# Six transformer blocks over eight sequences in one fused kernel: the up projection as three fp32r products, with new orders and PSUM banks on every engine

## What is computed

```
for i in range(DEPTH):                                   # 6
    x = attn_layer(shift_tokens(x), Wqkv[i], q_scale[i], k_scale[i], Wo[i]) + x
    x = ffn_layer(shift_tokens(x), ln_g[i], ln_b[i], W1[i], b1[i], W2[i], b2[i]) + x

def ffn_layer(x, g, bln, W1, b1, W2, b2):
    xn = (x - mu) / jnp.sqrt(var + 1e-05) * g + bln
    hg = xn @ W1 + b1                                    # 128 -> 2 x 341, the up projection
    a, gate = jnp.split(hg, 2, -1)
    return a * jax.nn.gelu(gate, approximate=False) @ W2 + b2
```

## Time and profile before

| | |
|---|---|
| median of 3 runs | 1501.54 us (1500.04 to 1501.63) |
| span of the profiled execution | 1500.0 us |
| PE busy | 1464.2 us (98%) |
| DVE, ACT, POOL busy | 1310.1 (87%), 1267.7 (85%), 1248.7 (83%) us |
| PE's share of the chain that ended last | 93% |
| granted TensorE clock, mean over the span | 0.995 |

### The profile page before, as it was taken

The page is one execution under the profiler, slowest core; times in us unless marked ns, Lnnn a source line. Parts: engine busy times, 40 slices in busy tenths (PEclk is TensorE's granted clock), DMA queues, the critical chain, the costliest instruction groups (busy, mean ns, idle before and its releaser), DMA issues.

```text
span 1500.0 us, 66306 instructions
## 1 busy us (share of the span) xinstructions
PE 1464.2 (98%) x26320; PEld 1280.8 (85%) x26320; DVE 1310.1 (87%) x2365; ACT 1267.7 (85%) x2551; POOL 1248.7 (83%) x1213
## 2 busy tenths in 40 slices
PE   6799999999999999999999999999999999999997
PEld 5578888888888888888888888888888888888886
DVE  6799998889889898888898898889898988998974
ACT  4578888889888888888898888888888888888886
POOL 5489988888888888888888888888888888888781
PEclk9899999999999999999999999999999999999999
DMA  6012212111212111121211121211112121112111
GB/s 185 22 46 60 59 46 57 43 49 42 59 49 79 52 47 43 54 63 52 70 41 50 43 70 49 69 45 50 47 40 55 52 54 38 49 35 52 38 49 39
DMA packets 96184, 80.28 MB, mean 54 GB/s; under 512 B 66282, under 2 KB 79598, under 8 KB 95854
## 3 DMA queue, kind: packets, MB, share of 16 engines
q1 hardware_dynamic: 94990, 75.34, 18.8%
q10 hardware_dynamic: 864, 0.26, 0.1%
HBM read 17.91 MB, written 1.05 MB: 13 GB/s over the span
## 4 chain that ended last, share of the span: by engine, by line
PE 93%; issue 2%; DVE 2%; POOL 1%; ACT 1%; DMA 0%; ACTq 0%; DVEq 0%; POOLq 0%
PE bank L1065 74%; PE bank L1179 11%; PE bank L1217 6%; PE bank L1251 1%; PE bank L1149 1%; DMA rot<-in_b_v 0%; POOL rot L459 0%; DVE parts L891 0%; DVE newton L910 0%; DVE s L937 0%; DVE n L901 0%; DVE am L825 0%; POOL w_lo L446 0%; ACTq L550 0%; ACT rot L576 0%
## 5 line engine op out<-in xcount | busy, mean ns | idle before, releaser
L459 POOL TENSOR_TENSOR rot<-parts 128x512 f32<-128x512 f32 x384 | 493.3, 1285 | 120.4 <-DVE parts L891 120.3
L891 DVE TENSOR_TENSOR parts<-bank,rtab 128x1024 f32<-128x1024 f32 x384 | 459.8, 1208 | 0.4 <-POOL rot L459 0.3
L470 POOL TENSOR_TENSOR rot<-rot,rnorm 128x512 f32<-128x512 f32 x384 | 391.1, 1046 | 10.0 <-DVE rnorm L917 10.0
L901 DVE TENSOR_REDUCE n<-sq 128x8 f32<-128x512 f32 x384 | 257.7, 671 | 33.0 <-ACT sq L627 33.0
L689 ACT ACTIVATE pz<-bank 64x512 f32<-64x512 f32 x384 | 226.1, 589 | 61.4 <-PE bank L1217 59.1
L1065 PE MATMUL bank<-w_hi,x_hi 128*128 128x512 f32 x576 | 263.8, 458 | 4.6 <-DVE parts L891 3.6
L476 POOL TENSOR_TENSOR es<-es,r 128x512 f32<-128x512 f32 x192 | 202.6, 1055 | 75.2 <-DVE r L943 75.2
L627 ACT ACTIVATE sq<-bank 128x512 f32<-128x512 f32 x384 | 230.4, 601 | 28.0 <-DVE n L901 22.0
L1065 PE MATMUL bank<-w_hi,x_lo 128*128 128x512 f32 x576 | 229.5, 398 | 0.0
L1065 PE MATMUL bank<-w_lo,x_hi 128*128 128x512 f32 x576 | 229.1, 398 | 0.0
L1179 PE MATMUL bank<-ident,rot 128*128 128x128 f32 x1536 | 203.1, 275 | 5.0 <-POOL rot L470 2.4
(11 more groups left out here) (86 smaller groups left out, 2660.4 us busy)
## 6 DMA issues: line engine op xcount, KB each, us to landing
vb<-v SPq DMA_DIRECT2D x96, 384.0 KB, 3.8
w_new<-in_Wqkv SPq DMA_DIRECT2D x36, 256.0 KB, 4.2
vb<-v SPq DMA_DIRECT2D x48, 128.0 KB, 3.4
w_o<-in_Wo SPq DMA_DIRECT2D x12, 256.0 KB
xin<-x_tok SPq DMA_DIRECT2D x48, 64.0 KB, 2.1
xs<-x_tok SPq DMA_DIRECT2D x48, 64.0 KB, 2.0
xin<-x_tok SPq DMA_DIRECT2D x48, 56.0 KB, 2.7
xs<-x_tok SPq DMA_DIRECT2D x48, 56.0 KB, 2.0
```

The lines of the kernel that those rows point to most:

```text
L459: g.tensor_tensor(rot[:, i * CH:(i + 1) * CH].rearrange(halves, z=2, c=HD), parts[:, b:b + CH].rearrange(halves, z=2, c=HD), parts[:, b + ...
L470: g.tensor_tensor(c, c, over(r, CHH, DH), ALU.mult).then_inc(s_sc[i], 1)
L891: d.tensor_tensor(parts[:, b:b + 2 * CH].rearrange("p (w h c) -> p w h c", w=2, c=DH), heads(bank[QK_BANK[i]][:, :]).unsqueeze(1).to_broad ...
L901: d.tensor_reduce(n2[:, T * 2 * HEADS + m * CHH:T * 2 * HEADS + (m + 1) * CHH], heads(sq[:, b:b + CH]), op=ALU.add, axis=AX.X).then_inc(s_ ...
```

## The change

- The input of `hidden` is split: ACT writes xg_hi (rounded to fp32r) with `affine`, and then the same affine once more in full precision into the free half of the bank (`affine2`); DVE subtracts (`xg_lo_part`, writes xg_lo). `hidden` runs three fp32r products in the place of each fp32 product.
- W1 is loaded into w_new, and split once a layer: ACT `split_up` (w1_hi) and, for the first layer POOL, later DVE (w1_lo). There is one buffer of each for all layers. The loads of Wqkv chunks 0 and 1 come in another order around it.
- Every engine's `iteration(n)` is listed in another order, with other lags (`finish` and two of the gelus come one iteration later, DEEP is 7), and the bank tables are other ones. The counts of all other operations in a step are as before.
- PE's stream is aligned twice a step, ahead of `hidden` chunk 0 (offset 72) and ahead of `project(n, 2)` (offset 77).

```
-DEEP = 5
-BLOCK, SLOT = 256, 92
-SPLIT_FROM = 2
+DEEP = 7
+BLOCK = 256
+SPLIT_FROM = 1
...
-        w_1 = sb("w_1", 2 * 2 * HID)
+        w1_hi = sb("w1_hi", 2 * HID, F32R)
+        w1_lo = sb("w1_lo", 2 * HID, F32R)
...
+            def up_weights(l):
+                if l < DEPTH - 1:
+                    sp.wait_ge(s_wl, (l + 1) * WCH + 2 if l else 2)
+                else:
+                    sp.wait_ge(s_upl, l)
+                sp.dma_start(w_new[:, 0:2 * HID], W1[l * P:(l + 1) * P, :]).then_inc(s_up, 16)
...
-            for c in range(WCH):
+            up_weights(0)
+            for c in (2, 3, 4, 5, 0, 1):
                 qkv_weights(1, c)
...
+            def split_up(l):
+                act.wait_ge(s_up, 16 * (l + 1))
+                for j in range(HCH):
+                    act.wait_ge(s_hid[j], l * SEQS)
+                a.activation(w1_hi[:, :], w_new[:, 0:2 * HID], ACT.Copy).then_inc(s_uph, 1)
...
             def affine(n):
                 act.wait_ge(s_xnt, done(n))
                 for j in range(HCH):
                     act.wait_ge(s_hid[j], done(n - 1))
+                act.wait_ge(s_xg, n)
                 l = layer(n)
-                a.activation(xg[:, :], bank[N_BANK][:, 0:LEN], ACT.Identity, bias=shift[:, l:l + 1],
-                             scale=gain[:, l:l + 1]).then_inc(s_xg, 1)
+                a.activation(xg_hi[:, :], bank[N_BANK][:, 0:LEN], ACT.Identity, bias=shift[:, l:l + 1],
+                             scale=gain[:, l:l + 1]).then_inc(s_xgh, 1)
+
+            def affine2(n):
+                l = layer(n)
+                act.wait_ge(s_xnt, done(n))
+                a.activation(bank[N_BANK][:, LEN:2 * LEN], bank[N_BANK][:, 0:LEN], ACT.Identity, bias=shift[:, l:l + 1],
+                             scale=gain[:, l:l + 1]).then_inc(s_xgf, 1)
...
+            def xg_lo_part(n):
+                dve.wait_ge(s_xgh, done(n))
+                dve.wait_ge(s_xgf, done(n))
+                d.tensor_tensor(xg_lo[:, :], bank[N_BANK][:, LEN:2 * LEN], xg_hi[:, :].bitcast(F32), ALU.subtract)\
+                 .then_inc(s_xg, 1)
...
             def hidden(n, j):
 
                 pe.wait_ge(s_xg, done(n))
+                if n % SEQS == 0:
+                    pe.wait_ge(s_upl, layer(n) + 1)
                 for half in range(2):
-                    w = (par(n) * 2 + half) * HID + j * P
-                    last = mm(bank[H_BANK[j]][0:width(j), half * LEN:(half + 1) * LEN], w_1[:, w:w + width(j)], xg[:, :])
+                    w = slice(half * HID + j * P, half * HID + j * P + width(j))
+                    o = bank[H_BANK[j]][0:width(j), half * LEN:(half + 1) * LEN]
+                    mm(o, w1_hi[:, w], xg_hi[:, :], stop=False)
+                    mm(o, w1_lo[:, w], xg_hi[:, :], start=False, stop=False)
+                    last = mm(o, w1_hi[:, w], xg_lo[:, :], start=False)
                 last.then_inc(s_hid[j], 1)
```

More of the change, by code:

```diff
@@ L369, in later_weights @@
                     sp.wait_ge(s_xready, n)
-                for part in ((0,), (1,), (2,), (3, 4), (5, 6), (), (), ())[k]:
+                for part in ((0,), (1,), (2, 3), (4, 5), (), (), (), ())[k]:
                     weights(l, part)
             def later_qkv(n):
[L375 to L379, removed]
+                l, k = n // SEQS, n % SEQS
+                if k == 2 and l > 0:
+                    up_weights(l)
+                for c in ((), (), (), (2,), (3,), (4,), (5, 0), (1,))[k]:
+                    if l + 2 < DEPTH:
+                        qkv_weights(l + 2, c)
+            sp.wait_ge(s_zero, 3)
             def iteration(n):
@@ L961, in moments, with up_lo @@
                     d.bn_aggr(mv[:, T * 2:(T + 1) * 2], stat[:, T * 6:(T + 1) * 6]).then_inc(s_mv, 1)
+            def xg_lo_part(n):
[3 more added lines that the diff above has]
+                 .then_inc(s_xg, 1)
+            def up_lo(n):
+                if n % SEQS == SEQS - 1 and layer(n) < DEPTH - 1:
+                    dve.wait_ge(s_uph, layer(n) + 2)
+                    d.tensor_tensor(w1_lo[:, :], w_new[:, 0:2 * HID], w1_hi[:, :].bitcast(F32), ALU.subtract)\
+                     .then_inc(s_upl, 1)
             def gated(n, j):
@@ new lines, in iteration @@
+                    project_v(n - 2, 2)
+                if live(n - 1):
+                    freed((s_qte[5], n - 2), (s_rot[1], n - 1, 8, 3))
+                    project(n - 1, 7)
+                    freed((s_qte[6], n - 2), (s_rot[0], n - 1, 8, 2))
+                    project(n - 1, 6)
+                if live(n - 2):
+                    freed((s_mid[0], n - 3), (s_sub[0], n - 2, 4, 0))
+                    turn_qk(n - 2, 7)
+                if live(n):
+                    freed((s_v[3], n - 2), (s_rot[1], n - 1, 8, 1))
+                    take_in(n)
@@ new lines, in iteration @@
+                if live(n):
+                    freed((s_xl, n))
+                    project(n, 1)
+                if live(n - 2):
+                    freed((s_mid[1], n - 3), (s_qte[4], n - 2))
+                    turn_p(n - 2, 0)
+                    freed((s_pte[1], n - 2, 4, 1))
+                    freed((s_rot[1], n - 1, 8, 5), (s_pte[0], n - 3, 4, 2))
+                    scores(n - 2, 1)
+                    freed((s_rot[0], n - 1, 8, 6), (s_qte[6], n - 2))
+                    values(n - 2, 1)
+                    freed((s_rot[1], n, 8, 1), (s_v[3], n - 2))
+                    values(n - 2, 0)
@@ new lines, in iteration @@
+                if live(n - 1):
+                    freed((s_hm[0], n - 5), (s_qte[7], n - 2))
+                    project_v(n - 1, 1)
+                if live(n):
+                    freed((s_sub[1], n - 2, 4, 3), (s_rot[1], n - 1, 8, 5))
+                    project(n, 0)
+                if live(n - 5):
+                    freed((s_hm[1], n - 5))
+                    down(n - 5)
+                if live(n - 1):
+                    freed((s_pte[0], n - 2, 4, 0))
+                    turn_qk(n - 1, 1)
+                    freed((s_ot[1], n - 2), (s_rot[0], n - 1, 8, 6))
+                    turn_qk(n - 1, 2)
@@ L1369, in iteration @@
[L1369 to L1379 removed]
+                    freed((s_xready, n - 5), (s_v[2], n - 2), (s_rot[0], n - 1, 8, 4))
```

514 lines of the change are left out of this document (240 added, 274 removed).

## The result

The changed kernel takes 1657.06 us (median of 4 runs, 1653.82 to 1660.17) against 1501.17 us for the kernel before beside it (1500.04 to 1501.63). The ratio is 1.1035 with a 95% interval of 1.1021 to 1.1049: 10% slower, where 2% faster was forecast, and outside the range. The profiled execution has a span of 1654.4 us, 154.4 more than before.

What follows compares the result with a forecast made beforehand. PE's list was taken as the bound: a step of 29.56 us less 0.40 (up projection) and 0.30 (small runs) is 28.86; 47 steps save 32.9 us, the ends add 0.5 and 1.6, giving 1471 us, 8 in 10 within 1452 to 1492.

Steps and rivals of the forecast that it cites:

- What bounds the kernel now: Mid-program steps: PE is busy in all of 29.56 us, so the time changes first with the sum of PE's list.
- The sum: Whole kernel: step 28.86 us, 47 steps gain 32.9 us, start and drain add 0.5 and 1.6; time 1471 us.
- The second alignment: PE's sequencer: one more branch, costed at nothing because it stands behind large products.
- The split of W1: ACT and DVE, five times: about 0.8 us each, covered, so nothing; up to 15 us if the cover is gone.
- Rival (a): PE begins to wait in the steps under the new lists: 0.3 us a step lost, 1485 us; chance 0.16.
- Rival (b): DVE round trip from affine to gated leaves 0.9 us or more of PE open a step: 1499 to 1530; chance 0.10.
- (c): In hidden, fp32r at 256 columns streams no faster than an fp32 pass, 0.216 us each: 1550 us; chance 0.05.
- (d): In hidden, weight loads don't overlap the products, 0.30 us each: 1617 us; chance 0.01.
- The up projection on PE: hidden on PE: 18 fp32r products at 0.122 us replace 2.60 us; -0.40 us a step, ends -0.60 and -0.30.
- The edges of runs of small products: Scores and values joined on PE save switches between large and small products: -0.30 us a step, ends -0.54 and -0.12.
- Start and drain: Program's two ends: 0.5 us more at the start, 1.6 us in the drain, 5 us either way for new orders.

Runs made afterwards that it cites:

- the repaired version: Changed kernel with W1's load ahead of load_xs, one alignment a step at offset 20, and take_p(n-3, 0) ahead of gelu chunk 2: 1501.79 us.
- The versions on the lists of before: Kernel before, its lists kept, with fp32r products in hidden alone (no splitting): 1478.89 us; with the whole split of input and W1: 1493.85 us.
- The version with the longest stops: Changed kernel with both alignment offsets 40 higher (112 and 117), nothing else: 1750.29 us in a single run.

## Why the prediction was wrong, by its steps

**What bounds the kernel now: right, but read as if it would stay so.** The step was PE's own list, with no waits. That is a statement about one order and one set of block edges, not about the work. The sum took it over to lists that share neither.

**The second alignment, "so I cost the second at nothing": the step that failed worst.** The reason I gave, that it stands behind large products, looked only at the branch itself, and the branch was indeed hidden. But an alignment also fixes where all later edges of the step fall, and for that the sum had no term. Together with the joined run, which I had costed only for its edges between sizes, it made 400 small instructions with two edges in them, the second of which PE reached before its block was there: 85.6 us of stops. Going to one alignment at 20 gave 87 us; with one at 72, 130 us came back; with the old lists and a moved SLOT, 83 us were lost. None of my rivals had it. The page of before gave no sign of it: of the 2% "issue" in the chain of the earlier trace rows some 28 us lie in the first 140 us and 4 us between the fifth and the last take_in. What could be read beforehand was the length of the joined run, from the order.

The Trainium skill (Runtime: NRT & Kernel Launch, section Instruction fetch mechanics) says that instructions come in 16 KiB blocks of 256 and that the fetch is hidden, since instructions are dispatched more slowly than the blocks fill. The size agrees with 4.72 MB in 288 packets. The rest disagrees with this trace: in the stop shown above 256 small matmul instructions took 2.6 us, and the next block was there 4.7 us after the edge.

**The split of W1, "Nothing, then; if that cover is gone, up to 5 x 3 = 15 us": failed, bound included.** I looked at the room between two `hidden` for the split, about 20 us, and on SP only at who waits for take_in. Who waits for the load of W1 itself I never asked. It stands behind load_xs, whose wait for `middle` holds the queue up to 15 us, and it reaches ACT's list, strictly in order. Measured: 9.5 us five times, of which 35 us came back. With the load in a better place a layer change costs 1.0 to 1.6 us more than another step.

**Rival (a), PE begins to wait: right in kind, wrong in place, size and chance.** I set the DVE chain from `scores` to `turn_p` against it. What waits is `values(n-2, 0)` in PE's list, for `take_p(n-3, 0)` in ACT's (the same step, one iteration later in that list), behind a gelu and a table load: 33 us, some 0.7 a step, where I had 0.3. Rival (b), the DVE round trip to xg_lo, did not happen: two waits, 3.5 us in all, in the last of the repaired versions, both at the end. (c) and (d) fell by the spacing of `hidden`. Timeline of PE in the changed kernel, which answers to the earlier trace rows:

```profile
735.39 0.60 PE L1276 MATMUL bank<-ident,es 128*128 128x128 f32 x4
735.75 0.36 PE L1124 MATMUL bank<-xg_hi,w_hi 128*128 128x256 f32 x1
735.95 0.28 PE L1124 MATMUL bank<-xg_hi,w_lo 128*128 128x256 f32 x1
736.07 0.28 PE L1124 MATMUL bank<-xg_lo,w_hi 128*128 128x256 f32 x1
...
737.25 0.40 PE L1124 MATMUL bank<-w_hi,x_hi 128*128 128x512 f32 x1
```

**The up projection on PE: right, a little too careful.** Eleven products take 735.95 to 737.25, 0.118 each; I took 0.122, between 0.111 and 0.128. The first one costs nothing extra: with the four transposes ahead of it it takes 0.56 us (735.39 to 735.95), which is 4 x 0.111 + 0.118. The term measured alone is -0.50 a step for -0.40, inside the ends. The 0.109 that I had estimated by the Trainium skill (TensorE: Matmul & The Clock Gate, section Back-to-back issue gap), which calls this the gap of an isolated matmul, without a budget for the load, is lower than any spacing in mid-program in these traces, the least of which is 0.112.

**The edges of runs of small products: right in sign, too large.** Inside the joined run above, kt,qt to pz,vb takes 783.76 to 785.15, 1.39 us, which is what kt,qt took with its full exit in the earlier trace rows. So the seam costs the exit and saves the entry of the next; to it comes the pause of 0.10 that a first values product has anyway. With the lists of before and -0.50 from `hidden` a step is 29.01 to 29.07, with the joined runs 28.9 to 29.1: that leaves 0.0 to 0.15 for this term, not 0.30. The joined run that was to bring it is also the one that ran dry.

**The sum.** The three edits (W1's load, one alignment at 20, take_p) give back 35, 87 and 33 us, 155 of the 186 us between my 1471 and the result. With them the typical step is 28.9 to 29.1 for my 28.86, but the mean is 29.18, so a step gains 0.39 us where I had 0.70: the hidden term held, the term of the small runs did not, and layer changes and the longer steps take the rest. The other 31 us are 14 us in these steps, 7 us ahead of the fifth take_in and 10 us behind the last.

**Start and drain: the size was off.** I had 0.5 + 1.6 and a range of 5. In the repaired version it is 5.0 ahead of the fifth take_in and 11.2 behind the last. The versions on the lists of before separate the sources of the latter: the shorter products of `hidden` take 1.5 us off the end (88.4 to 86.9), the splitting adds 6.5 (93.4), and the new orders 6.3 (99.7).

**What stays open.** Which of the reordered pieces makes the end of the repaired version longer was not tried. Outside the layer changes seven of its steps take 29.3 to 29.9. Each holds a stop of 0.2 to 0.5 us inside bank<-ident,rot, again 2.4 to 2.6 us behind the start of a packet, and each layer change a wait of 0.9 us for take_p on ACT; the rest of their excess is unexplained. That it is the fetch of the block that runs dry rests on the moved edges, which the stops followed, and on the packets, which start at about the same distance ahead of PE's going on; no record names the cause of a stop, and what starts a packet is not shown.

## What to carry to other kernels

Count instructions between large operations as well as their time: in these runs a series of small matmuls that held a whole block of 256 instructions between two edges stopped the engine at the second, mostly by 0.5 to 2.5 us, and an alignment or any edit ahead of it moves the edges, so after each edit look for "issue" in the middle of a run, and try offsets before judging the edit. For each load that is moved on a queue in strict order, ask who waits for that load and what the transfers ahead of it wait for. And put a new operation into the old lists first: here that version won, and the new lists around it lost up to 10%.

## What the runs showed of the hardware that I had not expected

- The instruction stream comes in packets of 16 KB, 256 instructions. 256 small matmul instructions last 2.6 us in the joined run; PE could go on only 3.3 to 5.3 us after the edge before, and in all 373 stops 2.2 to 3.3 us after the start of a packet. Edges at a bad place cost 83 us in the kernel before, 130 us in the repaired one.
- A branch over padding, mostly 0.2 to 0.4 us on PE's queue, takes longer the sooner it comes after an edge: medians of 0.38, 1.8 and 3.4 us at some 134, 94 and 54 instructions behind it, 3.9 us at most. Only the last showed in PE's time.
- Stops of 2.1 us between small products can be followed by products at half speed (0.43 us for 0.23 at 512 columns; granted 0.83 over 10 us). The version with the longest stops lost more than their length: 93 us against the changed kernel for 54 us of stops more.
- fp32r products of 256 columns stand 0.118 apart, half of the 0.233 of 512 columns: their cost has hardly a fixed part.
